# Four experts' inputs made by selection products instead of a scatter, and gates, biases and row sums moved behind the experts

## The reference, cut to what matters

```
xn     = layer_norm(r)                         # 1024 tokens x 128, (xn * w + b) before an expert
p      = softmax(xn @ router)                  # 1024 x 16
m1, m2 = one-hot of the best and the second best expert of each token
rank   = running count of the tokens of an expert, all first choices ahead of all second choices
kept   = m * (rank <= 128)                     # an expert takes at most 128 tokens
G      = 0.8 * p * (kept1 + kept2) / sum       # gates
x     += sum over the two choices of G * (gelu(xn_e @ fc1 + b1) @ fc2)
x     += G @ b2                                # the second biases, weighted by the gates
```

## Time and profile before

| | |
|---|---|
| runs | 1166.42, 1168.15, 1169.07 us |
| profiled execution: time | 1169.73 us |
| its span (first to last instruction) | 1167.9 us |
| PE busy | 928.1 us (79%) |
| DVE busy | 564.4 us (48%) |
| ACT busy | 439.4 us (38%) |
| POOL busy | 238.6 us (20%) |
| mean granted TensorE clock | 0.886 of full |
| DMA | 55.68 MB, mean 48 GB/s |

### The profile page before, as it was taken

One profiled execution on the slowest core, in us unless ns is written; L12 is line 12 of the kernel. 1 busy time (PEld: TensorE's weight loads), 2 busy tenths in 40 slices (PEclk: granted clock), 3 DMA queues, 4 the chain that ended last, 5 costly groups with the idle time before them and its releaser, 6 DMA issues. The chain is left out here.

```text
span 1167.9 us, 15202 instructions
## 1 busy us (share of the span) xinstructions
PE 928.1 (79%) x5428; PEld 624.8 (53%) x5433; DVE 564.4 (48%) x1251; ACT 439.4 (38%) x769; POOL 238.6 (20%) x274
## 2 busy tenths in 40 slices
PE   6886699634746629999876968999699988879998
PEld 4663345324634416777745952223256676747776
DVE  5875446253226471211656758676154447731111
ACT  2341446432322104334343323676432233433443
POOL 0551301034053100000354542201000012320110
PEclk9995979857977857999888996999899989978999
DMA  8014410313620000111000032410001110000111
GB/s 334 1 37 100 129 30 19 137 63 108 187 79 1 1 0 1 37 37 35 1 1 1 1 91 46 123 42 3 1 27 30 38 37 1 1 1 19 37 37 37
DMA packets 33263, 55.68 MB, mean 48 GB/s; under 512 B 3697, under 2 KB 25398, under 8 KB 32817
## 3 DMA queue, kind: packets, MB, share of 16 engines
q1 hardware_dynamic: 32176, 52.86, 14.8%
q0 software_dynamic: 1024, 1.98, 0.6%
HBM read 44.79 MB, written 9.96 MB: 47 GB/s over the span
## 5 line engine op out<-in xcount | busy, mean ns | idle before, releaser
L2302 PE MATMUL psum<-xT_all,wexp 128*128 128x512 f32 x400 | 184.3, 606 | 1.2 <-issue 0.7
L1505 DVE TENSOR_REDUCE arena<-psum 128x2 f32<-128x1024 f32 (+3 forms) x128 | 127.2, 1021 | 79.6 <-PE psum L2088 49.9
L1047 ACT ACTIVATE arena<-psum 128x512 f32<-128x512 f32 (+3 forms) x256 | 116.0, 515 | 85.8 <-PE psum L2101 48.3
L740 POOL TENSOR_TENSOR rstd<-var,held 128x8 f32<-128x8 f32 (+3 forms) x22 | 46.1, 2116 | 384.6 <-DVE var L1258 358.2
L2302 PEld LDWEIGHTS psum<-xT_all,wexp 128*128 128x128 f32 x400 | 74.4, 195 | 78.6 <-issue 73.6
L2317 PEld LDWEIGHTS psum<-wexp,arena 128*128 128x128 f32 x800 | 95.9, 195 | 14.9 <-issue 14.8
L2085 PE MATMUL psum<-arena 72*128 72x512 bf16 (+3 forms) x256 | 82.6, 394 | 25.6 <-DMA arena<-parts_q 12.4
L2013 PE MATMUL psum<-values_out_all,arena 128*128 128x128 f32 x560 | 77.3, 286 | 26.6 <-ACT arena L1011 26.5
L2317 PE MATMUL psum<-wexp,arena 128*128 128x128 f32 x800 | 96.2, 278 | 0.0
L815 POOL TENSOR_TENSOR arena<-arena,small 128x616 f32<-128x616 f32 x56 | 67.9, 1215 | 126.4 <-DVE small L1435 126.2
L2013 PEld LDWEIGHTS psum<-values_out_all,arena 128*128 128x128 f32 x560 | 68.1, 194 | 36.3 <-ACT arena L1011 34.9
(11 more groups left out here) (292 smaller groups left out, 1400.0 us busy)
## 6 DMA issues: line engine op xcount, KB each, us to landing
wexp<-experts SPq DMA_DIRECT2D x24, 514.0 KB, 3.6
parts_k<-wexp SPq DMA_DIRECT2D x12, 384.0 KB, 2.9
arena<-parts_k SPq DMA_DIRECT2D x48, 96.0 KB
arena<-parts_q SPq DMA_DIRECT2D x48, 96.0 KB
arena<-experts SPq DMA_DIRECT2D x8, 514.0 KB, 3.7
arena<-rows SPq DMA_DIRECT2D x8, 512.0 KB, 8.8
wexp<-experts SPq DMA_DIRECT2D x9, 384.0 KB, 3.1
held<-packed SPq DMA_DIRECT2D x1, 2375.0 KB, 15.6
```

What stands on the lines that cost most here:

```text
L740: pool.tensor_tensor(dst, src, half[0:src.shape[0], 0:n], ALU.pow).then_inc(done, 1)
L1047: act.activation(p_self[:, n % 2, kt % 2, j, lo:S], bank(t_bank("keys", c, k), lo, S), ACT.Exp, scale=DS ** -0.5).then_inc(ut_ok, 1)
L1505: dve.tensor_reduce(top[:, x % 2, qt, j:j + 2], src, AX_X, ALU.max, negate=True).then_inc(us_ok, 1)
L2302: mm(bank(c, 0, BANK), wexp[:, side, c * P:(c + 1) * P], xT_all[:, b * S:(b + 1) * S], start=True, stop=True).then_inc(h_ps, 1)
```

## The change

Rows are numbered by the kernel after where they differ.

- The experts 0 to 3 no longer get their inputs from `queued`. DVE keeps, for each token and expert, the rank if the expert takes the token and 0 if not (`ranks`: two instructions after `slots_ok`). For each of the four experts DVE compares the ranks of the eight tiles with the numbers 1 to 128 (`selected`, a new constant `places` of 128 columns in the first piece of `held`). The result (`chosen`, 128 x 1024 ones and noughts, two buffers) is the moving operand of eight accumulating products with the tokens as the stationary one; they give the turned queue at once, in place of the transpose.
- The scatter itself is unchanged: 16 indirect DMAs. SP waits for it only after the weights of experts 4 and 5 were loaded and the answers of 0 and 1 stored, and then loads the queues of experts 4 to 7.
- `run_queues` writes its first four steps out and loops twice instead of three times. The order of the steps on PE is the same as before.
- Gates, biases (in PSUM banks 6 and 7 in place of 0 to 3) and row sums are behind the experts: on DVE gates, `own_values(1)`, row sums, biases' sum, then the gathered answers; on PE biases after `prep(1)`; on ACT the copy of the turned gates after `prep(1)`. ACT's squares move ahead of the gelu table load, straight behind the exponential of the gating. POOL's inverse norms move into layer 1.

```diff
@@ run_queues @@
-            for e in range(-max(ahead for _, ahead in lagged), 0):
+            for e in range(-max(ahead for _, ahead in lagged), 4):
                 steps(e, e, 0)
-            with eng.Fori(0, E0 // 4 - 1) as i:
+            with eng.Fori(0, E0 // 4 - 2) as i:
@@ sync @@
-            sp.wait_ge(scattered, 16 * 16)
-            for side in range(4):
-                load_queue(side, side)
+            for e in range(4):
+                if e == 2:
+                    sp.wait_ge(scattered, 16 * 16)
+                    for side in range(4):
+                        load_queue(4 + side, side)
+                sp.wait_ge(d_O, e + 1)
+                load0(e + 4, e)
+                store_answer(e, e)
@@ gpsimd: queues, layer 1 @@
-                inverse_norms()
...
                 elif l == 1:
+                    inverse_norms()
@@ scalar @@
+                if l == 0:
+                    for e in range(8):
+                        act.wait_ge(n_in, 16 * 8)
+                        act.activation(rows3[:, e, :], rows3[:, e, :], ACT.Square).then_inc(n_sq, 1)
+                    return
...
                 prep(1)
+                turned_gates(0)
@@ vector: gating(0) ends after slots_ok with @@
+                    step.then(dve.tensor_tensor(M["pre"], bank(0, 0, 2 * n), M["mk"], ALU.mult))
+                    step.then(dve.tensor_tensor(ranks, M["pre"][:, 0:n], M["pre"][:, n:2 * n], ALU.add))
+                    return
@@ vector: experts0 @@
+                def selected(e, side, i):
+                    if not isinstance(e, int) or e > 3:
+                        return
+                    if e > 1:
+                        dve.wait_ge(d_T, e - 1)
+                    dve.tensor_tensor(chosen[side % 2].rearrange("p (t c) -> p t c", c=P),
+                                      w("places").unsqueeze(1).broadcast_to([P, NT, P]),
+                                      ranks.rearrange("p (t e) -> p t e", e=E0)[:, :, bass.ds(e, 1)].broadcast_to([P, NT, P]),
+                                      ALU.is_equal).then_inc(d_hot, 1)
+
+                run_queues(dve, (selected, 3), (features, 2), (answer, 0))
+                gates0()
+                own_values(1)
...
+                add_biases(0)
@@ tensor: experts0 @@
+                def queue(e, side, i):
+                    if not isinstance(e, int) or e > 3:
+                        pe.wait_ge(d_in[side], i * 16)
+                        pe.wait_ge(d_xe, e + 1)
+                        turn(bank(side % 2, 0, P), D["xin"][:, side * P:(side + 1) * P], ident).then_inc(d_T, 1)
+                        return
+                    pe.wait_ge(d_hot, e + 1)
+                    pe.wait_ge(d_xe, e + 1)
+                    for t in range(NT):
+                        last = mm(bank(side % 2, 0, P), xn_moe[:, t * P:(t + 1) * P], chosen[side % 2][:, t * P:(t + 1) * P],
+                                  start=(t == 0), stop=(t == NT - 1))
+                    last.then_inc(d_T, 1)
-                run_queues(pe, (turned, 2), (hidden, 1), (output, 0))
+                run_queues(pe, (queue, 2), (hidden, 1), (output, 0))
                 prep(1)
+                biases(0)
```

More of the change, by code:

```diff
@@ L270, in program @@
         D = take(dict(past_M=12032, w=2 * 1028, xin=4 * P, xe=2 * P, h=2 * 512, y=4 * P, back=16 * P, loc=256, slot=64))
+        ranks, row_sums = M["diag"][:, 0:P], M["diag"][:, P:P + 64]
+        chosen = [D["back"][:, n * 1024:(n + 1) * 1024] for n in range(2)]
         W0 = [wexp[:, 0, :], wexp[:, 1, :], D["w"][:, 0:1028], D["w"][:, 1028:2056]]
@@ L345, in program @@
         WB = [[0, 0], [0, 0], [4, 4], [9, 8]]
[L347 removed]
+        GB, BB = [6, 6, 6, 6], [6, 6, 6, 6]
         XT = [2, 4, 2, 2]
@@ L1806, in experts0 @@
                 dve.tensor_scalar(s2_col, s2_col, 1e-24, None, ALU.max).then_inc(n_max, 1)
-                run_queues(dve, (features, 2), (answer, 0))
-                own_values(1)
+                add_biases(0)
                 for n in range(2 * NT):
@@ L2272, in gating, with biases @@
                        start=False, stop=True, skip_group_check=True).then_inc(g_loc, 1)
[L2273 to L2285 removed]
+                elif l != 2:
+                    biases(l)
+            def biases(l):
+                E_ = MOE[l]["E"]
+                n = [1, 2, 0, 3][l]
+                pe.wait_ge(gate_ok, n)
+                for t in range(NT):
+                    last = turn(psum[0:E_, GB[l] * BANK + t * P:GB[l] * BANK + (t + 1) * P], gates[:, t, 0:E_], ident)
+                last.then_inc(gT_ps, 1)
+                pe.wait_ge(gT_ok, n)
+                for t in range(NT):
+                    last = mm(psum[:, BB[l] * BANK + t * P:BB[l] * BANK + (t + 1) * P], gatesT[0:E_, t * P:(t + 1) * P],
+                              w(f"m{l}_b2"), start=True, stop=True)
+                last.then_inc(b2_ps, 1)
+                if l == 0:
+                    pe.wait_ge(b2_ok, n)
             def experts(l):
@@ L2329, in experts0 @@
             def experts0():
-                def turned(e, side, i):
-                    pe.wait_ge(d_in[side], i * 16 + 16)
+                def queue(e, side, i):
[5 more added lines that the diff above has]
+                    pe.wait_ge(d_hot, e + 1)
                     pe.wait_ge(d_xe, e + 1)
-                    turn(bank(side % 2, 0, P), D["xin"][:, side * P:(side + 1) * P], ident).then_inc(d_T, 1)
+                    for t in range(NT):
+                        last = mm(bank(side % 2, 0, P), xn_moe[:, t * P:(t + 1) * P], chosen[side % 2][:, t * P:(t + 1) * P],
+                                  start=(t == 0), stop=(t == NT - 1))
+                    last.then_inc(d_T, 1)
                 def hidden(e, side, i):
```

81 lines of the change are left out of this document (40 added, 41 removed).

## The result

The changed kernel takes 1176.1 us (median of 6, 1173.9 to 1182.2) where the kernel before takes 1168.3 (median of 6, 1166.4 to 1169.1): ratio 1.0083 over all runs, interval 1.006 to 1.0106 (the two medians alone give 1.0067). It is 7.8 us slower; 9.3 us faster had been forecast. The profiled execution took 1173.9 us.

The account below looks back on a forecast made before the run. Path taken as gating, scatter, experts paced by loads, gather, layer 1. Experts' gain 9.5 less opening 0.2 gives 9.3 us less: median 1168.15 to 1158.9 us, range 1155.8 to 1163.2.

Parts of the forecast that it names:

- The cover holds with 0.8 us to spare: Behind the experts: gates, sums and biases finish before the gather's last rows at 339.1, so the moves cost nothing.
- rival 3: Behind the experts: moved work ends after the gather, overrun 2 to 5 us, time 1161 to 1164; chance 0.08.
- SP issues at 272.37 and PE turns at 274.20: After the scatter: first queue load and turn come as before, now for expert 4, PE idle 6.3 us.
- The scatter keeps its 16 issues and its start: Layer 0's scatter on POOL: unchanged beside the selections, so queue loading starts no later.
- rival 2: Layer 0's scatter: slowed by selections or weight loads, up to 4.9 us, gain 4.4, time 1163.8; chance 0.08.
- Experts: 9.5 us: Layer 0's experts: queue 8 turned at 287.2 instead of 296.70, and the 9.5 us gain stays through the loop.
- Opening: 0.2 us: Kernel start: the first piece of `held` is 10% larger and lands 0.2 us later, at most 0.6.
- Rival 4: Gather on POOL: stretched 15.1 us by DVE's work beside it, 5.8 us slower, time 1174; chance 0.04.
- Rival 1: First four experts: selection stays cold or late, queue 4 turned 4.3 us late, time about 1162; chance 0.10.
- rival 5: Experts: clock outlasts the 6.3 us pause or loads come sooner, gain 11.3, time 1156.8; chance 0.08.

Follow-up runs that it names:

- Queues first: Changed kernel with SP waiting for the scatter and loading queues 4 to 7 before output 1 and expert 5's weights: 1162.86 us (chip 6), 1173.12 us (chip 1).
- the chain in it: Kernel before with a second, unused copy of the biases' chain beside the gather, DVE waiting for it: 1178.19 us, ratio 1.009 (chip 6).
- moves alone: Kernel before with gates, biases, row sums behind the experts, squares ahead, norms in layer 1, no selection: ratio 1.0068 (chip 3), 1.0091 (chip 1).
- plain gather: Changed kernel with 16 plain SP transfers replacing POOL's 16 indirect gathers: ratio 0.9913 (chip 6), 0.9884 (chip 13), 0.9947 (chip 3).

## Why the prediction was wrong

The step that failed is *"The cover holds with 0.8 us to spare"*: the tail was put at nothing and cost 11.1 us. Under it, and under SP's issue of the queues, lies one assumption: that whoever needs a product of PE gets the signal when it ends. I took it from the earlier trace rows, where PE works beside the indirect transfers for 7 to 8 us and is prompt. The change has PE work beside them from the scatter's first issue on, with DVE, ACT and SP all waiting for it, and on chips 1 and 3 it isn't prompt (on 3 as its variants show). On which chip the pair of the result ran is not known; the trace of after has the late signals, and its ratio of 1.0083 agrees with the changed kernel's on chip 1 (1.0066).

- *"The cover holds with 0.8 us to spare"* failed by 11.1 us. This is rival 3 in kind (the tail opens), outside its bounds: it had 2 to 5 us, because I priced PE's and ACT's work and not the time until it is known. On chip 13 the step is right: biases' sum made at 333.97, 16.1 us behind the last answer where 19.8 were forecast, and the rows added at +25.1.
- *"SP issues at 272.37 and PE turns at 274.20"*: 24.4 us behind the release became 29.3. Of these 4.9, 1.4 are the scatter's (below), 2.0 are SP's wait for output 1's late signal, 1.5 the queues' landing behind the weights of expert 5. The forecast has output 1 ended at 267.9, 4.5 us before SP needed it, so standing in line for it was to cost nothing. Queues first bears the 3.5 us out (3.3 less on chip 1). On chip 13 it was 25.7, late by the scatter alone.
- *"The scatter keeps its 16 issues and its start"* was off by 1.4 us. The first scatter took 1997 ns where 1199 was the longest before, and ended just as the two selections did; one beside selection 4 took 1.51 us. The selections are the reason: in every trace with them the longest scatter took 1996 to 2023 ns and the last was issued 21.2 to 22.1 us behind the release, in the five without them (the kernel before on two chips, the chain in it, moves alone twice) 1199 or 1200 ns and 20.4. It is rival 2 with a smaller price: not 4.9 but 1.4. The stricter reading of the Trainium skill, "SBUF — State Buffer", section "Who interferes with whom", is partly borne out: descriptor generation beside a DVE instruction with two SBUF inputs was stretched, in two of the 16, never by more than the length of one such instruction; that it is spared, as the page infers, the trace doesn't show.
- *Experts: 9.5 us.* 4.4 were measured: 9.5 less 4.9, and about 0.2 in the loop. On chip 13 it was 6.1: queue 8 turned 8.3 earlier than before, but experts 8 to 15 took 29.9 us instead of 27.6; the granted clock was 0.83 to 0.86 between 285 and 305 us, where the kernel before had 1.00 from 284 to 324, and outputs 8 and 12 took 1.91 us instead of 1.06. That the gain would stay in the loop was thus a second, smaller miss. It varies: the plain gather on the same chip, the same program up to there, had its last answer at +66.2, a gain of 8.6.
- *Opening: 0.2 us.* Not seen: the release came 2.7 us earlier here and 0.7 on chip 13, and over all traces with a scatter it lies between 247.0 and 252.0; a difference of 0.2 disappears in that spread.
- *Rival 4, the one with the right sign*, had the wrong mechanism: the gather kept its pace beside DVE's sums (last issue at +21.2 after 21.3, issues 0.94 to 1.00 us). *Rival 1*: the selection was not late, its clock rose earlier than I had put it (0.93 in 251.6 to 258.5).
- *The range* doesn't follow from its own words: rival 5 ends at 1156.8, and the middle of rival 2's loss is 1158.9 + 2.45 = 1161.3, not 1155.8 and 1163.2. Nothing of the failure hangs on it.

With prompt signals the size was nearly right: on chip 13 the changed kernel's span is 7.7 us shorter (0.7 at the start, 6.1 in the experts, 1.0 in the first 25 us of layer 1), its median 1161.9, inside the range of 1155.8 to 1163.2. In part that is luck: 1.7 of the 7.7 us lie where the forecast had nothing, and the experts gave 6.1 of their 9.5.

What wasn't settled: by what path POOL's transfers hold PE's signals up, what differs between the chips (each but 3 was seen in one group only, so the time of the group could matter as well), and whether one that shows late signals always does (chip 3 did in both groups, 7 of 7 profiles; chip 1 in 3 of 3; chips 6 and 13 in none of 7).

## What to carry to other kernels

Keep work that depends on PE's signals out of the stretch in which POOL's indirect DMAs are in flight, or place it so that nothing on the path waits before they end: the kernel with queues first, gates in the pause and biases among the experts loses nothing on late chip 3 (0.9984) and gains a little on the others (0.9963, 0.9971), where the changed kernel swings between 0.9935 and 1.0066 (1.0083 in the result above). "Hidden behind a transfer" has to be asked in signals too: a chain of PE, ACT, PE, DVE needs three of them, two of PE. And a change that wins by half a per cent is to be timed on more than one chip before it is called faster or slower.

## What the runs showed of the hardware

- On two of four chips a semaphore update of PE arrived 3 to 12 us after its product had ended (output 0: ended 259.19, copied 267.01; layer 1's values: 326.71 and 333.47, 327.29 and 339.12), while POOL's indirect DMAs were in flight; in the kernel before, on such a chip, 2.4 and 2.7 us. Several pending updates then came together: in the changed kernel three of them (features, hidden, output 1) within 0.2 us at 272.1, about 1 us after the scatter had landed. Plain DMAs issued by SP in place of the gather, with the same sizes, didn't do it.
- PE itself shows gaps without a releaser meanwhile: the eight records of output 1 lie between 263.90 and 267.78 us, where on chip 13 such eight took 1.06 us.
- One and the same program differed by 14 us in its median between chips (1175.7 and 1161.9), while the kernel before differed by 1.4.
- With a chain added that cost nothing at its place, the rest of the same program took 10 us longer, at a granted clock of 0.66 instead of 1.00 in one stretch of 15 us; that the chain caused it is not shown.
- The longest scatter on POOL took 1996 to 2023 ns in every trace in which it ran beside DVE instructions of 1.2 us with two inputs in SBUF, 1199 or 1200 ns in the others.
